# A decoder layer on one core: normalisations written as a two-tensor operation, a shorter expert gate, and every engine's order laid anew

## The reference

```python
x = layernorm(x + self_attention(x))          # 16 heads of 8; (q k)/sqrt(8), causal, polymax in place of softmax
x = layernorm(x + cross_attention(x, ctx))    # 16 heads of 64, softmax, WO and a bias
x = layernorm(x + experts(x))                 # 16 experts of 128x128, the 6 likeliest of each token
# polymax(s) = (s*s + 1)/1000 for s > 0, (1 - s/100)/1000 for -100 <= s <= 0, else 0
# layernorm(x) = (x - mean) / sqrt(var + 1e-5)
probs = softmax(x @ router_w.T + router_b)    # experts: [T, 16]
top_p, top_i = top_k(probs, 6)
top_p = top_p / (sum(top_p) + 1e-10)
gate  = scatter(top_p at top_i)               # [T, 16], zero elsewhere
acc   = max(sum(gate), 1e-10)
out   = sum over e of (x @ expert_w[e]) * gate[:, e] / acc + 1e-10 * sum(top_p)
```

## Time and profile before

| | |
|---|---|
| time, median of 3 runs | 1192.78 us |
| lowest and highest of them | 1187.5 and 1199.39 us |
| span of the profiled execution (first to last instruction) | 1184.6 us |
| time of the profiled execution itself | not among the three; with what lies around the span it is a little longer than it |
| busy, of the span | PE 95%, DVE 94%, PE weight loads 73%, ACT 65%, POOL 62% |

### The profile page before, as it was taken

How to read it: one execution, slowest core, us unless ns; L and a number is a source line. 1 busy time by engine, 2 the same in 40 slices (tenths; PEclk the granted TensorE clock), 3 DMA queues, 4 the chain that set the end, 5 groups by cost and what they waited for, 6 DMA issues and landing times.

```text
span 1184.6 us, 30898 instructions
## 1 busy us (share of the span) xinstructions
PE 1126.7 (95%) x9472; PEld 867.1 (73%) x9472; DVE 1112.7 (94%) x2699; ACT 770.0 (65%) x1578; POOL 736.9 (62%) x776
## 2 busy tenths in 40 slices
PE   6999999999999999999999999999999999999973
PEld 5878777778777777777777777777877777877752
DVE  4789999999999999999999999999999999999886
ACT  4886767666767766677766677766676766676430
POOL 4235566666556666656666656666666666765666
PEclk9999999999999999999999999999999999999996
DMA  4333223333233333222333222333222333322230
GB/s 148 96 94 69 58 63 90 93 93 77 51 72 79 93 93 84 53 73 68 93 93 93 57 70 58 93 93 93 65 63 64 87 93 93 77 53 63 71 77 13
DMA packets 49998, 92.09 MB, mean 78 GB/s; under 512 B 6576, under 2 KB 28592, under 8 KB 49968
## 3 DMA queue, kind: packets, MB, share of 16 engines
q1 hardware_dynamic: 49968, 91.70, 30.7%
HBM read 20.37 MB, written 4.19 MB: 21 GB/s over the span
## 4 chain that ended last, share of the span: by engine, by line
PE 46%; DVE 33%; issue 17%; DVEq 1%; POOL 1%; ACT 1%; DMA 1%; SPq 0%; POOLq 0%
PE ps_B L368 36%; DVE weighted L754 7%; PE ps_S L368 5%; PE ps_B L476 5%; DVE x L698 5%; DVE p L741 3%; DVE allowed L730 3%; DVE rowmax L709 3%; DVE kp_lo L826 2%; DVE poly L736 2%; DVE stats L676 2%; DVE r L839 1%; DVE mv L682 1%; DVEq L246 1%; DVE rowsum L718 0%
## 5 line engine op out<-in xcount | busy, mean ns | idle before, releaser
L904 POOL TENSOR_TENSOR weighted<-weighted 128x1024 f32<-128x1024 f32 (+3 forms) x256 | 313.3, 1224 | 103.5 <-DVE weighted L754 100.5
L890 POOL TENSOR_TENSOR p<-p,rowinv 128x1024 f32<-128x1024 f32 x64 | 122.9, 1920 | 194.3 <-DVE rowinv L722 194.3
L542 ACT ACTIVATE z<-ps_B 128x512 f32<-128x512 f32 x256 | 149.7, 599 | 118.2 <-PE ps_B L368 115.3
L754 DVE TENSOR_TENSOR weighted<-ps_B,gate 128x512 f32<-128x512 f32 x256 | 171.8, 684 | 14.7 <-PE ps_B L368 9.5
L368 PE MATMUL ps_B<-cT_hi,a_hi 128*128 128x256 f32 x512 | 156.0, 305 | 1.5
L698 DVE TENSOR_SCALAR x<-r,mv,rstd 128x128 f32<-128x128 f32 x192 | 152.5, 835 | 2.9 <-POOL rstd L885 2.9
L542 ACT ACTIVATE vb_raw<-ps_B 128x512 f32<-128x512 f32 x256 | 147.4, 590 | 5.4 <-PE ps_B L368 3.0
L368 PE MATMUL ps_B<-cT_hi,a_lo 128*128 128x256 f32 x512 | 144.6, 282 | 0.0
L368 PE MATMUL ps_B<-cT_lo,a_hi 128*128 128x256 f32 x512 | 144.6, 282 | 0.0
L368 PE MATMUL ps_B<-vo_hi,cT_hi 128*128 128x512 f32 x256 | 112.7, 440 | 16.4 <-DVE kp_lo L826 10.5
L368 PEld LDWEIGHTS ps_B<-vb,p2T 128*64 128x64 f32 x2048 | 110.6, 137 | 23.4 <-issue 23.2
(11 more groups left out here) (110 smaller groups left out, 2785.3 us busy)
## 6 DMA issues: line engine op xcount, KB each, us to landing
vb<-vb_raw SPq DMA_DIRECT2D x256, 256.0 KB, 4.3
xT<-in_x_t SPq DMA_DIRECT2D x32, 256.0 KB, 2.6
cT<-in_ctx_t SPq DMA_DIRECT2D x32, 128.0 KB, 2.2
x_sb<-in_x SPq DMA_DIRECT2D x32, 128.0 KB, 2.2
out<-x SPq DMA_DIRECT2D x32, 128.0 KB, 1.9
weighted<-in_wq_t SPq DMA_DIRECT2D x1, 512.0 KB, 4.2
weighted<-in_wk_t SPq DMA_DIRECT2D x1, 512.0 KB, 5.6
weighted<-in_wv_t SPq DMA_DIRECT2D x1, 512.0 KB, 6.9
```

The source lines that it names most:

```text
L542: return nc.scalar.activation(dst, src, ACT.Copy, scale=scale)
L754: V.tensor_tensor(weighted[:, r, 512 * q:512 * q + 512].rearrange("p (e c) -> p e c", e=4), ps[BANK[job]][:].rearrange("p (e c) -> p e c", ...
L890: G.tensor_tensor(weights, weights, rowinv[:, r].unsqueeze(2).broadcast_to([P, H, T]), ALU.mult).then_inc(p2_ready, 1)
L904: G.tensor_tensor(a, a, b, ALU.add).then_inc(add_steps, 1)
```

## The change

It has three parts. First, the layer norms' `(x - mean) * root` and the addition of 1e-5 to the variance are no longer written with `tensor_scalar` but with operations that read two tensors: the root is read as a second tensor whose one column is repeated 128 times, and 1e-5 stands in a tile of its own. Second, the gate works on the exponentials without dividing them by their sum first; the sum enters through the small constants instead, and 16 steps stand for 20. Third, all five orders and the banks are new. A small part more: the sum AC waits for fewer semaphores, only for the last job of each bank.

```diff
-GATE_STEPS = 20
-GEPS_STEP = 16
+GATE_STEPS = 16
+GEPS_STEP = 14
...
-    V.tensor_scalar(rstd[:, n - 1], mv[:, n - 1, :, 1], LN_EPS, None, ALU.add).then_inc(ln_eps[n - 1], 1)
+    V.tensor_tensor(rstd[:, n - 1], mv[:, n - 1, :, 1], ln_eps_tile[:], ALU.add).then_inc(ln_eps[n - 1], 1)
...
-    V.tensor_scalar(dst[:, r], src[:, r], mv[:, n - 1, r, 0:1], rstd[:, n - 1, r:r + 1], ALU.subtract, ALU.mult).then_inc(done, 1)
+    V.scalar_tensor_tensor(dst[:, r], src[:, r], mv[:, n - 1, r, 0:1], rstd[:, n - 1, r:r + 1].broadcast_to([P, C]), ALU.subtract, ALU.mult).then_inc(done, 1)
...
-    nc.scalar.activation(logit[:], logit[:], ACT.Exp).then_inc(logit_exp_ready, 1)
+    nc.scalar.activation(prob[:, :, 0:E], logit[:], ACT.Exp).then_inc(logit_exp_ready, 1)
...
+def latest(jobs, waited=()):
+    order = [job for job, _, _ in JOBS]
+    return [job for job in jobs if BANK[job] not in waited and job == last_of(order, [other for other in jobs if BANK[other] == BANK[job]])]
...
-    wait_emptied(pe, i, f"PT{r}a")
-    wait_emptied(pe, i, f"PT{r}b")
+    for job in latest((f"PT{r}a", f"PT{r}b"), [BANK["AC1"]]):
+        wait_emptied(pe, i, job)
```

The gate's steps from the second on, before and after (the two lines of each pair in order; `max`, `memset` and `match_replace` stay and have other numbers):

```diff
-  2 lsum = reduce(logit)    3 linv = 1/lsum    4 prob = logit * linv    7 tsum = reduce(best)    11 tsum += TOP_EPS
-  12 gate = prob - left    13 tinv = 1/tsum    14 gate *= tinv    15 gsum = reduce(gate)    16 geps = gsum * TOP_EPS
-  17 gsum = max(gsum, TOP_EPS)    18 ginv = 1/gsum    19 gate *= ginv
+  2 lsum = reduce(prob)    5 tsum = reduce(best)    9 tall = lsum * TOP_EPS + tsum    10 gsum = max(tall * TOP_EPS, tsum)
+  11 gate = prob - left    12 tinv = 1/tall    13 ginv = 1/gsum    14 geps = tsum * TOP_EPS * tinv    15 gate *= ginv
```

Of the orders the diff shows the end of TensorE's list (the jobs from X2T on, and the first three of the next turn):

```diff
-    ("X2T", "B1", "l2"), ("FF5", "B5", "ff"), ("VB5", "B2", "l1"), ("LG", "B1", "l2"),
-    ("S2_0", "S", "l2"), ("Q", "B0", "s1"), ("K", "B4", "s1"),
+    ("X2T", "B2", "l2"), ("Z4", "B1", "l1"), ("LG", "B0", "l2"), ("Z6", "B2", "l1"), ("VB5", "B0", "l1"), ("VB6", "B3", "l1"),
+    ("S2_0", "S", "l2"), ("Q", "B1", "s1"), ("K", "B0", "s1"),
```

More of the change, by code:

```diff
@@ L78 @@
 SP_ORDER = """
-    x_columns place0 store context x_rows place1
+    x_rows x_columns context store place1 place0
 """.split()
 ACT_ORDER = """
-    Q K queries_hi0 VB0 exp0 Y queries_hi1 VB1 V VB3 product_hi0 VB4 relu0 Z7 square0 Z1 exp1 Z5 VB2 PT0a
-    PT0b relu1 product_hi1 product_hi2 square1 Z2 VB7 PT1b product_hi3 PT1a Z4 relu2 square2 product_hi4 Z3
-    Z0 base3 Z6 X1T relu3 product_hi5 X2T square3 VB6 product_hi6 VB5 logit_exp product_hi7
+    Q K queries_hi1 Y exp0 VB4 V queries_hi0 VB0 VB1 VB3 Z5 relu0 Z1 square0 Z7 VB2 exp1 PT0b PT0a relu1 Z2 VB7
@@ L85 @@
+    square1 PT1b PT1a base3 relu2 X1T Z0 square2 relu3 Z3 X2T square3 Z6 Z4 logit_exp VB6 VB5 product_hi0
+    product_hi1 product_hi2 product_hi3 product_hi4 product_hi5 product_hi6 product_hi7
 """.split()
 DVE_ORDER = """
[L87 to L89 removed]
@@ L90 @@
-    gate17 gate18 gate19 weigh1 product_lo3 weigh0 weigh3 p1_1 weigh2 stats3 var3 norm1 allow2 product_lo4
-    attended stats2 eps3 var2 eps2 weigh6 pieces2 norm2 weigh7 norm3 p1_2 product_lo5 weigh4 allow3 pieces3
-    logits gate0 p1_3 product_lo6 product_lo7 gate1 weigh5
+    row_max0 gate2 less_max0 gate3 keys_lo0 gate4 queries_lo gate5 keys_lo1 gate6 projected gate7 row_sum0 row_max1
+    gate8 stats1 gate9 row_inv0 gate10 less_max1 gate11 allow0 gate12 pieces0 gate13 row_sum1 gate14 row_inv1 gate15
@@ L93 @@
+    p1_0 allow1 weigh3 var1 pieces1 weigh1 eps1 stats3 p1_1 weigh0 weigh2 norm1 attended var3 stats2 allow2 var2
+    weigh4 eps2 weigh6 pieces2 norm2 eps3 p1_2 allow3 logits pieces3 gate0 norm3 weigh7 gate1 weigh5 p1_3
+    product_lo0 product_lo1 product_lo2 product_lo3 product_lo4 product_lo5 product_lo6 product_lo7
 """.split()
 POOL_ORDER = """
-    context_hi context_lo q_hi q_lo add1.0 shares0 add1.1 add1.2 experts_hi next_x_hi shares1 next_x_lo
-    add1.3 root1 add1.4 add0.0 root2 experts_lo root3 add0.1 bias_x1 add0.2 x2_hi add0.3 x2_lo add0.4
+    context_hi q_hi context_lo q_lo add1.0 add1.1 shares0 add1.2 shares1 add1.3 add1.4 root1 next_x_hi add0.0 root2
@@ L97 @@
+    add0.1 add0.2 bias_x1 root3 x2_hi x2_lo next_x_lo add0.3 add0.4 experts_hi experts_lo
 """.split()
@@ L793, in gate_step @@
                     if k == 11:
-                        return V.tensor_scalar(tsum[:], tsum[:], TOP_EPS, None, ALU.add)
+                        return V.tensor_tensor(gate[:], prob[:, :, 0:E], left[:, :, 0:E], ALU.subtract)
                     if k == 12:
-                        return V.tensor_tensor(gate[:], prob[:, :, 0:E], left[:, :, 0:E], ALU.subtract)
+                        return V.reciprocal(tinv[:], tall[:])
                     if k == 13:
-                        return V.reciprocal(tinv[:], tsum[:])
```

44 lines of the change are left out of this document (18 added, 26 removed), and 24 rows, old and new, of the table JOBS.

## The result

The changed kernel takes 1317.66 us (median of 4 runs, 1316.51 to 1320.15) against 1192.98 us (4 runs, 1187.5 to 1199.39) for the kernel before: ratio 1.1035, 95% interval 1.0972 to 1.1099. The prediction said slower, and by 2.4%; it is slower by 10.4%, far outside the range.

The account below looks back on a forecast made before the run. VectorE and TensorE, both at their limit and handing each other work, were taken as the bound. A turn of 36.4 us gave +33 over 29 turns, start and end -5: span 1212.6, plus 8.2 makes 1221 us; range 1158 to 1240.

Parts of the forecast that it names:

- The loop through VectorE: Waits once round a turn, Q to queries_lo to second norm to next Q: 36.4 us taken, 1.14 more than before.
- TensorE, with 34.56 at most, has slack: Matrix engine over a turn: busy 34.56 us at most, so not what sets the longer predicted turn.
- the second half gets in: Rival, first norm: its second half starts before GpSimd's add0.0 locks it; turn 35.05 us, 1182 us; chance 0.20.
- Two tensors do not collide: Rival, VectorE: two-input operations never wait for GpSimd, TensorE bounds the turn at 34.2 us, 1157 us; chance 0.13.
- The locks fall where VectorE is early: Rival: VectorE reaches queries_lo after add1.0 and loses nothing there; turn 35.3 us, 1189 us; chance 0.12.
- The norm's form: Norms and 1e-5 addition on VectorE: two-tensor form waits for GpSimd as before and is as long; nothing gained.
- The gate: VectorE between queries_lo and second norm: 11 gate steps instead of 16 there, -1.5 us a turn (bounds -1.0 and -2.0).
- Start and end: Scores ahead of the products at the start, -4 us; four gate steps fewer per tile at the end, -1 us.
- From span to median: Run median lies 8.2 us above the profiled span; added to the predicted span of 1212.6 us.

Follow-up runs that it names:

- both moves: Changed kernel with SyncE's place0 moved to mid-turn and ScalarE's evictions of VB6 and VB5 put ahead of the gate's exponentials: 1235.67 us, ratio 1.0372.
- (C): Theory that the norm's form itself costs or helps: changed kernel with old norms and 1e-5 addition, 1311.54 us; kernel before with new ones, 1209.49 us.

## Why the prediction was wrong

**The step that failed** is "SyncE: `place1` and `place0` now follow each other at the end; their data is wanted when ScalarE moves the next VB4 and VB0, and by my count lands just ahead of what then matters. Nothing, up to 1 us a turn if it is late." Measured: late by 2.64 and 1.57 us in the two waits of the turn shown, 4.4 us a turn on average (135.9 us over 31 turns). It cost 2.64 us of the turn (38.71 against 36.07) and 82 us of the run, of which `place0`'s place alone has 52. I had followed the transfers forward, to who wants them, and not back round: what releases `place1` is the eviction of VB6 and VB5, which now stand behind the gate's exponentials, and these behind everything VectorE does in the turn. Eight transfers in a row then take 6.3 us to issue and 5.1 to land. That a transfer might be late had no chance of its own among the rivals, though SyncE's list was in front of me; the last sentence, that ScalarE was taken as never late, names the hole and gives it no price.

**The loop through VectorE was right in its lengths, and only partly in its path.** It can be checked in the kernel with both moves, whose locks are those of the changed kernel. TensorE's X2T and the first Q behind it, and VectorE:

```profile
704.78 0.44 PE L498 MATMUL ps_B<-const,x 128*128 128x128 f32 x2 [0.72 <-DVE x L705]
...
710.36 0.39 PE L374 MATMUL ps_B<-xT_hi,w_qk_hi 128*128 128x256 f32 x1
```

```profile
677.72 4.15 DVE L819 TENSOR_TENSOR qm_lo<-q_lo,const 128x2048 fp32r<-128x2048 f32 x1
...
702.86 1.87 DVE L705 SCALAR_TENSOR_TENSOR x<-r,mv,rstd 128x128 f32<-128x128 f32 x2
...
713.82 4.15 DVE L819 TENSOR_TENSOR qm_lo<-q_lo,const 128x2048 fp32r<-128x2048 f32 x1
```

| piece of the turn | before | predicted | with both moves | changed kernel |
|---|---|---|---|---|
| Q to the end of `queries_lo` | 7.98 | 7.7 | 7.61 | 7.61 |
| to the end of the second norm | 22.75 | 22.9 or 23.45 | 22.86 | 25.4 |
| to the next Q | 4.30 | 5.45 | 5.63 | 5.63 |
| turn | 35.03 | 36.05 to 36.6 | 36.10 | 38.7 |

(The turn is 677.72 to 713.82; the second piece is from 681.87 to 704.73; the third to 710.36, and the first, from there to the end of `queries_lo` at 717.97. The last column is the turn of the changed kernel that begins with Q at 718.41, where `queries_lo` ends at 726.02, the second norm at 751.46, and Q comes at 757.09.) All of the excess stands in the second piece, where TensorE's VB2 waits for ScalarE and ScalarE for `place0`.

The chain that ended last in the kernel with both moves takes another way through the same turn:

```profile
668.68 0.44 PE ps_B L498 x2
...
693.88 0.34 DVE weighted L761
...
702.86 1.88 DVE x L705 x2
...
704.78 0.44 PE ps_B L498 x2
```

From X2T it follows TensorE's list for 25.20 us, until VectorE can take the product of `weigh1` at 693.88, and only the last 10.90 us, with the locks of norm 1 and norm 2, are VectorE's. `queries_lo` isn't on it; VectorE waits some 0.4 us for TensorE there, in each of 13 turns. That VectorE's own sum from `queries_lo` on came out as the length of the piece is because it has only these 0.4 us of slack. So "TensorE, with 34.56 at most, has slack" was wrong, and it is why freeing `queries_lo` gained nothing. In the kernel before it was much the same: the chain leaves VectorE behind `kp_lo` at 614.45, and comes back to it at 630.86.

**What of VectorE's locks was right and off.** `queries_lo` takes 4.15 us, said to be near 4.5. `gate<-prob,left` takes 0.92, some 0.7 of it lock, where 0.65 was counted. Norm 1's second half misses `add0.0` and the pair has 2.65 us of the chain, some 2.0 of it lock where 2.2 was counted, norm 2's 1.87, 1.2 of it lock where 1.25 was counted; the rival "the second half gets in" did not happen. "Two tensors do not collide" is refuted in both orders (C): the Trainium skill, "SBUF — State Buffer", section "Who interferes with whom", by which two SBUF inputs contend with GpSimd, agrees with the trace (mean 994 ns, least 339). "The locks fall where VectorE is early": half right for `queries_lo`, which could be freed of 1.9 us without gain, wrong for the norms, which without their locks give 57 us even there.

**The norm's form**, "nothing again", was right to 6 us for the changed kernel (1317.7 with the new, 1311.5 with the old) and is 17 us in the kernel before. The term was sized at the instruction, where 0.06 us is right, and not at the race it decides.

**The gate**, -1.5 us in its piece: alone it gave nothing; it can't be separated out in the new order, where the piece as a whole came out as summed.

**Start and end**, -4 and -1. The first score eviction came at 14.43 us, as said ("about 14"). But from the first `queries_lo` to the fourth it is 92.85 us (9.22 to 102.07) against 75.12 before, and from the last one to the end 129.0 against 112.0: +17.7 and +17.1 where I had -5 in all. With both moves they are still 90.4 and 124.1, that is +15 and +12. So of the 131 us of span between the two profiled runs, 97 us are the 28 turns in the middle (23 us are left of these with both moves), and 34 us the two ends. Start and end, taken as a gain of 5 us, are thus the second term that was mis-sized, by 39 us. The first mistake there was to look at the first wait only; what makes turns -1 and 0 long was not found. It is not the products' place. That the two groups of transfers have no other tile's work beside them there (the chain of the kernel with both moves has `place1`'s landing in it at 65.26, 5.56 us) is argued, not shown.

**From span to median**, 8.2 us. In the changed kernel's profiled execution only 2.0 us lie around the span (1317.38 against 1315.4). The other 6 of the 8.2 are that the profiled execution of before was a quick one of its kind, and the sum carried them over to a kernel for which nothing spoke for them.

## What to carry to other kernels

Follow a loop through every engine that may be late, SyncE included: for each transfer ask what releases it and what stands ahead of that in its engine's list, and give groups of transfers that share a queue their issue time in a row, not only their landing time. Before trusting a per-instruction cost, look whether that instruction starts within a tenth of a microsecond of GpSimd's: there the race decides, and an edit of 0.06 us moved the turn by 0.6. Ask the trace for the chain that ended last, over one turn, before naming the engine that sets it. And where VectorE is held up by GpSimd in small operations that read only SBUF, moving them to ScalarE paid here, 4.8% of the kernel, even at 0.49 us for 0.34.
